# Relative attention: the stores of the attention weights to DRAM are issued by the ACT queue instead of the SP queue

## What is computed

```python
rel_k = rel_k_table[_rel_idx(t, s)]
attn2 = jnp.einsum('bhqd,qkd->bhqk', rq, rel_k)
attn = jax.nn.softmax((attn1 + attn2) / scale, axis=-1)
w1 = jnp.einsum('bhqk,bhkd->bhqd', attn, rv)
rel_v = rel_v_table[_rel_idx(t, s)]
w2 = jnp.einsum('bhqk,qkd->bhqd', attn, rel_v)
x = (w1 + w2).transpose(0, 2, 1, 3).reshape(b, t, D_MODEL)
```

## Time and profile before

| | us |
|---|---|
| runs before the change, median of 3 | 2900.47 |
| lowest and highest | 2886.98 and 2901.21 |
| the profiled execution, its own time | 2904.39 |
| its span in the trace | 2902.7 |
| PE busy in the span | 2443.1 (84%) |
| DVE busy | 1547.8 (53%) |
| ACT busy | 1240.6 (43%) |
| POOL busy | 616.5 (21%) |

### The profile page before, as it was taken

One profiled execution on the slowest core, in us unless ns is written; L12 is line 12 of the kernel. 1 busy time (PEld: TensorE's weight loads), 2 busy tenths in 40 slices (PEclk: granted clock), 3 DMA queues, 4 the chain that ended last, 5 costly groups with the idle time before them and its releaser, 6 DMA issues. The chain is left out here.

```text
span 2902.7 us, 55677 instructions
## 1 busy us (share of the span) xinstructions
PE 2443.1 (84%) x19216; PEld 1940.2 (67%) x19216; DVE 1547.8 (53%) x2951; ACT 1240.6 (43%) x2780; POOL 616.5 (21%) x723
## 2 busy tenths in 40 slices
PE   8969999996899999939994899999999998496047
PEld 5648888886799999927773566666666666353035
DVE  5844555556411111138993556656666555544875
ACT  2212222221133333316662555555555555435743
POOL 1101111114544444324442111211112111000000
PEclk9979999996799999969996999999999998698569
DMA  2112122216299999930003555555555553111211
GB/s 76 45 52 52 51 55 57 51 41 233 83 339 342 346 346 341 310 107 1 0 0 70 132 119 123 121 126 116 126 127 120 123 121 75 50 68 51 85 57 40
DMA packets 386699, 346.64 MB, mean 119 GB/s; under 512 B 70578, under 2 KB 365004, under 8 KB 384588
## 3 DMA queue, kind: packets, MB, share of 16 engines
q1 hardware_dynamic: 374348, 329.03, 39.7%
q0 software_dynamic: 12288, 16.79, 2.6%
HBM read 258.72 MB, written 87.05 MB: 119 GB/s over the span
## 5 line engine op out<-in xcount | busy, mean ns | idle before, releaser
L1974 ACT COPY rel_probT<-rel_ps_t 121x400 f32<-121x400 f32 x384 | 196.2, 511 | 260.8 <-PE rel_ps_t L2192 260.8
L2192 PE MATMUL rel_ps_t<-rel_ident,rel_prob 100*121 100x100 f32 x1536 | 249.5, 286 | 31.0 <-ACT rel_probT L1974 30.7
L2192 PEld LDWEIGHTS rel_ps_t<-rel_ident,rel_prob 100*121 100x121 f32 x1536 | 197.9, 187 | 105.7 <-ACT rel_probT L1974 76.3
L1986 ACT ACTIVATE rel_prob<-rel_ps_s,rel_nmx 100x361 f32<-100x361 f32 x512 | 264.7, 580 | 5.0 <-DVE rel_nmx L2075 4.9
L1141 PEld LDWEIGHTS moe_ps_h<-moe_xeT,moe_w 128*128 128x128 f32 x2048 | 240.0, 193 | 5.1 <-issue 1.9
L1141 PE MATMUL moe_ps_h<-moe_xeT,moe_w 128*128 128x128 f32 x2048 | 240.6, 276 | 1.3 <-DVE moe_xeT L1306 1.3
L2075 DVE TENSOR_REDUCE rel_nmx<-rel_ps_s 100x2 f32<-100x722 f32 x256 | 232.8, 909 | 8.8
L1141 PE MATMUL moe_ps_y<-moe_w,moe_hT 128*128 128x256 f32 x1024 | 231.5, 379 | 0.0
L2705 PE MATMUL ffd_ps_y<-ffn_w_dT,ffd_oq 128*100 128x256 f32 x384 | 86.3, 386 | 145.6 <-DVE ffd_oq L2650 140.0
L1141 PEld LDWEIGHTS moe_ps_y<-moe_w,moe_hT 128*128 128x128 f32 x1024 | 189.6, 190 | 23.2
L1132 ACT ACTIVATE moe_hT<-moe_ps_h,moe_b 128x128 f32<-128x128 f32 x512 | 142.9, 376 | 140.5 <-PE moe_ps_h L1141 140.1
(11 more groups left out here) (427 smaller groups left out, 5221.9 us busy)
## 6 DMA issues: line engine op xcount, KB each, us to landing
moe_w<-in_L_ffn_w SPq DMA_DIRECT2D x128, 1024.0 KB
rel_scores<-rel_r_ext SPq DMA_DIRECT2D x32, 818.8 KB
rel_r_key<-rel_scores SPq DMA_DIRECT2D x32, 818.8 KB
rel_weights<-rel_prob SPq DMA_DIRECT2D x128, 204.7 KB
rel_by_dist<-rel_weights SPq DMA_DIRECT2D x32, 400.0 KB
mut_ctx_nat<-in_ctx SPq DMA_DIRECT2D x32, 363.0 KB
mut_ctx_T<-in_ctxT SPq DMA_DIRECT2D x32, 361.0 KB
rel_ctx_T<-in_ctxT SPq DMA_DIRECT2D x32, 361.0 KB
```

Of the source, the lines that this page charges most:

```text
L1974: nc.scalar.copy(probT[:, pg % 2, c], ps_pT).then_inc(s_t_sb, 1)
L1986: last = nc.scalar.activation(prob[:, t.parity, slot, :], ps_s[0:S, j, 0:L], ACT.Exp, bias=nmx[:, slot:slot + 1])
L2192: last = nc.tensor.transpose(ps_pT[:, j, :], prob[:, pt.parity, QUAD * pg + j, c * STEP:c * STEP + R], ident[0:S, 0:S])
```

## The change

SP's four stores a turn are taken out; its wait before by_dist is now on one of two semaphores, by the parity of the batch. ACT issues the store of quad g in group g, after its third `probT` copy and ahead of the job at place 4g+3. Before quad 0 it waits, from the third batch on, for the by_dist that read the same half of the DRAM buffer two batches ago.

```diff
-        s_pout, s_pdist, s_far, s_far_sum = (sem("weights_in_dram"), sem("weights_by_distance"), sem("far_masked"),
+        s_pout, s_pdist, s_far, s_far_sum = ([sem(f"weights{v}_in_dram") for v in range(2)], sem("weights_by_distance"), sem("far_masked"),
...
-            def store(b, g):
-
-                sp.wait_ge(s_p, GROUPS * b.i + (g + 2))
-                sp.dma_start(p_rows[b.parity, :, QUAD * g:QUAD * (g + 1), REACH:PW],
-                             prob[:, b.parity, QUAD * g:QUAD * (g + 1), 0:NEAR]).then_inc(s_pout, 16)
-
             def turn(t):
                 b, nxt, prev, after = t, t + 1, t + -1, t + 2
-                if prev.within(B):
-                    store(prev, GROUPS - 1)
...
-                    sp.wait_ge(s_pout, 16 * GROUPS * prev.i + 16 * GROUPS)
+                    sp.wait_ge(s_pout[v], 16 * GROUPS * prev.half + 16 * GROUPS)
...
-                if b.within(B):
-                    store(b, 0)
...
-                if b.within(B):
-                    store(b, 1)
-                    store(b, 2)
...
-                    act.wait_ge(s_pout, 16 * GROUPS * (t.i - 1))
+                    act.wait_ge(s_pout[t.parity], 16 * GROUPS * t.half)
...
+            def store(b, g):
+                if not b.within(B):
+                    return
+                act.wait_ge(s_p, GROUPS * b.i + (g + 2))
+                if g == 0 and (not isinstance(b.i, int) or b.i > 1):
+
+                    act.wait_ge(s_pdist, 16 * (b.i - 1))
+                act.dma_start(p_rows[b.parity, :, QUAD * g:QUAD * (g + 1), REACH:PW],
+                              prob[:, b.parity, QUAD * g:QUAD * (g + 1), 0:NEAR]).then_inc(s_pout[b.parity], 16)
...
                     transposed(pt, pg, 2)
+                    store(t, g)
                     empty(t, 4 * g + 3)
```

## The result

| | before | after |
|---|---|---|
| median, 14 runs each | 2894.80 us | 2881.26 us |
| lowest and highest | 2886.98 to 2907.52 | 2876.16 to 2886.54 |
| ratio after / before, 95% interval | | 0.9948 [0.9936, 0.9960] |
| the profiled execution | 2904.39, span 2902.7 | 2876.16, span 2874.5 |
| mean turn of the loop, scores to scores | 26.89 (25 turns) | 26.41 (the same 25) |

Of the 11.2 us between the forecast (2892.5, unrounded) and 2881.26, 5.7 come from the base: the three runs shown had a median of 2900.47, the 14 now have 2894.80. The other 5.5 are the size of the gain, 13.5 us where 8 were forecast. As a ratio to the base that the prediction had, its lower end was 0.9943, and 0.9948 lies just inside it.

A forecast was written before the change was run, and what follows sets the result against it. PE was taken to bound the turn, SP costing only through by_dist's landing. -8 + 0 + 0 = -8 us gave 2896 profiled, 2892.5 (about 2893) on the median; own range 2886 to 2905, 8-in-10 range 2884 to 2980.

The forecast's parts named there:

- What bounds the kernel: Whole turn: PE sets it; SP's order costs only through DVE's by_dist wait; 25 turns carry 11.1 us above 26.45 each.
- So some 1.8 us of the wait is slack of DVE's: DVE's by_dist wait: a short turn held a wait of 1.82 us, so only what lies beyond some 1.8 costs.
- So by_dist is issued between 2008.0 and 2009.6 ... It starts 0.5 to 2.1 us earlier.: SP's by_dist issue: quad 3's store slowed 0 to 1.6 us by r_key; before, by_dist was handed over at 2010.13.
- the second rival: By_dist's landing: full engines, r_key ahead of quad 3's store, quad 0's beside by_dist; 1.0 us later, +27 us, 2927; chance 0.08.
- By_dist lands between 2.1 us earlier and 1.0 us later. I take 0.7 earlier.: By_dist's landing: earlier start against up to 1.5 us lost beside quad 0's store; 0.7 us earlier taken, engines not full.
- the signs: Expected traces if right: ACT stores about 0.3 us, r_key 2 to 3 us earlier, DVE's wait 1.7 to 1, turns near 26.5.
- With 0.7 us less, two thirds of the 11.1 us excess go, some 7 us in 25 turns, 8 over the stage.: PE's turns: by_dist landing 0.7 us earlier removes two thirds of their time above 26.45 us, giving -8 us.
- its upper case: PE's turns: the gain is bounded by the whole excess, 11.1 us plus a little outside the 25 turns, 13 in all.
- The issues on ACT, "costed at 0": ACT's four added issues a turn: 0.28 us each, all covered, quad 2 tightest with 0.48 us of cover; cost 0.
- ACT is held as SP was: Rival, ACT's store issues: ACT stands behind SP's transfers, 2.8 us a turn, +75 us, 2976; chance 0.32.
- By_dist lands later: Rival, by_dist's landing: full engines and stores ahead and beside make it 1.0 us later a turn, +27 us, 2927; chance 0.08.
- The whole excess goes, and more: Rival, PE's turns: by_dist 2.1 us earlier takes all 11 to 13 us, 2888; chance 0.17, including a draw at the edge.

## Why the prediction was wrong, step by step

**What bounds the kernel.** Right: the turn is PE's, SP's order costs only through by_dist, and 26.45 us is the length of a turn without that wait (26.41 now, and 26.41 without by_dist). Incomplete: the excess was counted from 1697.45 on, which left out the turn of 31.74 us just before, and PE's clock was read in one window at 1.00. A fall of the clock behind PE's stand was no term of the sum.

**"So some 1.8 us of the wait is slack of DVE's".** Misread. The wait of 1.82 us was given to a short turn, also in the earlier trace rows, the one that ends with the scores of 1910.76, but the d0 behind it stands in the next turn, of 26.91 us, and waits 0.22. The slack is 1.4 us.

**"So by_dist is issued between 2008.0 and 2009.6 ... It starts 0.5 to 2.1 us earlier."** This step failed, in both halves. The store of quad 3 took 7.3 us with r_key ahead, not 3.7 to 5.3; by the prediction's clock by_dist was issued at 2011.3 to 2011.4, and handed over 1.9 us later than before, not earlier. That alone would have made it land later, as the second rival had it. What it missed is that by_dist then has nothing beside it but the store of quad 0: 5.4 us from issue to landing instead of 9.7. R_key's rows are paid once, ahead of the store or ahead of by_dist, and the prediction added them to the store without taking them off by_dist.

**"By_dist lands between 2.1 us earlier and 1.0 us later. I take 0.7 earlier."** It landed 0.7 us earlier at the median of 25 turns, and DVE's wait fell from 1.7 to 0.9 us a turn, as the signs had it. That is luck: the start came out 1.9 us later instead of earlier, and the time from there to the landing 2.6 us shorter, and the two errors cancelled to the very number.

**"With 0.7 us less, two thirds of the 11.1 us excess go, some 7 us in 25 turns, 8 over the stage."** This is the term that was mis-sized. It shares out the excess in proportion to the wait. But only what lands beyond +11.84 costs, and there the 0.7 us takes nearly everything: with each landing of before 0.7 us earlier, 1.7 of the 9.3 us would be left (an estimate, from the 25 landings). After, 0.2 are left, since the latest landing moved by 1.1 us, and the clock no longer falls. So 12.0 us went in the 25 turns where 7 were forecast and 11.1 had been called the bound. The missing 1 us: even the short turns became 0.04 us shorter; why is not shown. Against the medians of the 14 runs the gain is 13.5 us, 15 by the ratio; the forecast said 8, and its upper case, 13 from the turns, is nearly what came.

**The issues on ACT, "costed at 0".** Right: 282 ns at the median, 564 at most, and all covered, at quad 2 as well.

**"ACT is held as SP was".** Wrong, at a chance of 0.32, and it drew the range up to 2980. For r_key's rows a queue pays for what is ahead of it in itself: the store of quad 3, 0.95 us behind r_key, takes 2.57 us in r_key's queue and 0.28 in the other. The Trainium skill, Perfetto Trace Analysis, section DMA Instruction — HWDGE (DVE, Sync), has issuing sequencers share the descriptor generator under a lock, with the wait in the issue. Here 128 issues on ACT between SP's transfers took at most 0.56 us, so nothing of the size that held SP is shared. (The 1.55 us of the second half at quad 2, on ACT, is the one hold that this leaves without a cause.) The same kernel could have shown this only with a DMA on another engine; before had none.

**"By_dist lands later".** Wrong for the change, but real: quads 0 to 2 alone do exactly this, with the stores of quads 0 and 1 beside by_dist. In the change the store of quad 0 costs by_dist some 0.7 us: 5.4 from issue to landing with it, 4.7 with quad 3 alone on ACT, where it stands behind (the 11 turns in which DVE waits). That r_key no longer stands directly ahead is worth more. The Trainium skill's sentence that several issuers share the 16 engines and only issue time is saved (DMA: Bandwidth & Descriptors, Issuing engines are not separate DMA queues) agrees with the runs in that the whole gain is to be had on SP alone. It says nothing of the order, and the order decided here: the same four stores, or a part of them, gave 0.9948, 0.9957 or 1.0087 by what stood ahead of by_dist and beside it.

**"The whole excess goes, and more", 0.17.** This is what happened, on the far side of its 2888, though not by the 2.1 us that it asked for. It was given too little: with a slack of 1.4 us, a landing 0.9 us earlier is enough for the long turn of the earlier trace rows and its wait of 2.25, and 1.2 us leaves 0.1 of the 9.3 (an estimate, from the same 25 landings). A steep saturation was taken for a proportional one.

## What to carry to other kernels

Before moving DMAs to another engine's queue, look for the one transfer that somebody waits for, and at what stands directly ahead of it in its own queue; here one block moved down in SP's order gave what the whole move gave, and three quarters of the move made the kernel 0.9% slower. If a move frees a transfer that had been held behind the critical one, ask what it will now run beside. To price an earlier landing, set it against the length of the turn for every turn and find the point from which it costs: below it a gain is worth nothing, above it all of it, and one turn picked out of 25 tells neither. And a stand of PE isn't only its own length: look at the granted clock behind it.

## What the runs showed of the hardware that was not expected

- An issue of 1600 rows (r_key) takes 0.28 us on SP and on ACT; the next issue in the same queue pays for it (2.39 on SP, 2.48 on ACT), and one in the other queue doesn't (0.28).
- Two stores of 200 rows back to back on ACT: the second takes 0.41 to 0.47 us at quads 0, 1 and 3 and 1.42 to 1.61 at quad 2, some 4.5 us behind SP's issue of the scores. That the scores make the difference is not shown.
- From a store of 400 rows to by_dist, which waits for it, passed 3.7 us with nothing ahead in any queue, 7.3 with 1600 rows ahead in the other and 8.8 with them ahead in its own.
- After a stand of 0.8 to 2.3 us PE's granted clock was at times 0.5 to 0.8 for 5 to 10 us; with the stand itself that made before's two turns of this kind 2.7 and 5.3 us longer.
